# Retention's weights behind the gathers, the residual rows normalised in retention, the router's scores made as columns

## The reference

```python
x = _layernorm(x + mamba(x)); x = _layernorm(x + cross_attention(x, ctx))
x = _layernorm(x + _L0_ffn_ref(x, ...))      # switch experts
x = _layernorm(x + _L1_attn_ref(x, ...))     # retention and feed-forward
...
def _L0_ffn_ref(inputs, Wr, br, W1, b1, W2, b2):
    logits = x @ Wr + br                     # 800 tokens, 8 experts
    probs = jax.nn.softmax(logits, axis=-1)
    gate, idx = jnp.max(probs), jnp.argmax(probs)
    pos = ...                                # place in the expert, capacity 100
    expert_in = gate * x[tokens of the expert]
    eo = relu(expert_in @ W1 + b1) @ W2 + b2
    return gate * eo[expert, place]
def _L1_attn_ref(x, ...):
    xn = _ln(x, norm1_w, norm1_b)
    q, k, v = xn @ wq + bq, xn @ wk + bk, xn @ wv + bv
    ret = ((q @ k.T) * Dmat) @ v             # by head, 16 heads
    h = (silu(xn @ wg + bg) * groupnorm(ret)) @ wo + bo
    x = x + h
    x2 = _ln(x, norm2_w, norm2_b)
    return x + (silu(u) * g @ w_out + b_out) # u, g halves of x2 @ w_in + b_in
```

## Time and profile before

| what | value |
|---|---|
| time, median of 3 runs | 2862.91 us (2861.91 to 2865.08) |
| time of the profiled execution | 2860.79 us |
| its span | 2858.7 us |
| PE busy | 2504.8 us (88%) |
| PEld busy | 1266.9 us (44%) |
| DVE busy | 1393.4 us (49%) |
| ACT busy | 897.5 us (31%) |
| POOL busy | 573.4 us (20%) |
| granted clock of PE, mean | 0.938 of 2.4 GHz |

### The profile page before, as it was taken

The page is one execution under the profiler, slowest core; times in us unless marked ns, Lnnn a source line. Parts: engine busy times, 40 slices in busy tenths (PEclk is TensorE's granted clock), DMA queues, the critical chain, the costliest instruction groups (busy, mean ns, idle before and its releaser), DMA issues. The chain is left out here.

```text
span 2858.7 us, 33018 instructions
## 1 busy us (share of the span) xinstructions
PE 2504.8 (88%) x12353; PEld 1266.9 (44%) x12353; DVE 1393.4 (49%) x1981; ACT 897.5 (31%) x1867; POOL 573.4 (20%) x490
## 2 busy tenths in 40 slices
PE   7899999988999999897289899885997669999994
PEld 4544444434555555545145454353664323333331
DVE  5788888721578886721325512285444521111113
ACT  3644544402533334401012110085333112212210
POOL 0055555500000000001401100000000033343343
PEclk9999999999999999998699899997998879999997
DMA  2022222136535544335510010112000151560633
GB/s 86 25 72 82 75 85 79 66 87 244 184 113 185 173 140 120 126 110 196 147 79 0 0 41 3 32 59 89 1 1 1 54 233 50 234 265 23 261 101 116
DMA packets 94622, 288.64 MB, mean 101 GB/s; under 512 B 26994, under 2 KB 57358, under 8 KB 80258
## 3 DMA queue, kind: packets, MB, share of 16 engines
q1 hardware_dynamic: 59378, 158.34, 16.6%
q0 software_dynamic: 35104, 128.36, 12.5%
HBM read 449.40 MB, written 47.11 MB: 174 GB/s over the span
## 5 line engine op out<-in xcount | busy, mean ns | idle before, releaser
L691 POOL TENSOR_TENSOR x_rows<-ms_state,mb_C_everywhere 128x800 f32<-128x800 f32 x128 | 241.4, 1886 | 312.2 <-DVE ms_state L668 181.9
L701 PE MATMUL psum<-ms_context,mb_key_w 128*128 128x361 f32 x768 | 269.1, 486 | 22.9 <-ACT x_rows L611 9.6
L922 PE MATMUL psum<-at_Wv,at_context 128*128 128x512 f32 (+1 forms) x576 | 266.1, 601 | 0.0
L668 DVE TENSOR_TENSOR_SCAN ms_state<-ms_decay,psum 128x800 f32<-128x800 f32 x128 | 232.1, 1814 | 57.5 <-ACT ms_decay L618 41.3
L2733 PE MATMUL psum<-tf_W,tf_x_T 128*64 128x512 f32 x1024 | 232.3, 601 | 8.9 <-DMA tf_W<-in_L_W,tt_weight_row 8.9
L2755 PE MATMUL psum<-tf_W,tt_hidden 128*64 128x512 f32 x1024 | 226.8, 595 | 0.0
L2788 ACT ACTIVATE tt_hidden<-psum,tf_b 128x64 f32<-128x64 f32 x512 | 112.1, 330 | 363.7 <-PE psum L2744 363.7
L701 PEld LDWEIGHTS psum<-ms_context,mb_key_w 128*128 128x128 f32 x768 | 136.3, 190 | 162.6 <-ACT x_rows L606 64.1
L2678 POOL DMA_INDIRECT tf_W<-in_L_W,tt_weight_row x128 | 127.2, 993 | 230.7 <-PE psum L2733 151.5
L1023 ACT ACTIVATE at_prob<-psum,at_neg_max 100x722 f32<-100x722 f32 x128 | 110.5, 864 | 145.7 <-DVE at_neg_max L1085 145.4
L1085 DVE TENSOR_REDUCE at_neg_max<-psum 100x1 f32<-100x722 f32 x128 | 115.5, 903 | 78.3 <-PE psum L943 77.9
(11 more groups left out here) (461 smaller groups left out, 3876.3 us busy)
## 6 DMA issues: line engine op xcount, KB each, us to landing
at_piece<-in_L_W_f POOLq DMA_DIRECT2D x24, 1024.0 KB, 6.2
keys_dram<-x_rows SPq DMA_DIRECT2D x128, 180.5 KB, 1.9
at_k_cols<-keys_dram SPq DMA_DIRECT2D x64, 361.0 KB, 3.1
sf_W<-in_L_W SPq DMA_DIRECT2D x16, 1024.0 KB, 6.9
tf_W<-in_L_W SPq DMA_DIRECT2D x8, 2048.0 KB, 27.0
ms_context<-in_ctxT SPq DMA_DIRECT2D x16, 541.5 KB, 4.3
at_context<-in_ctxT SPq DMA_DIRECT2D x8, 1083.0 KB, 5.3
ternary_dram<-at_piece_made POOLq DMA_DIRECT2D x14, 512.0 KB, 4.0
```

The lines of the kernel that those rows point to most:

```text
L668: nc.vector.tensor_tensor_scan(state[:, n % RH, :], decay[:, g % RA, :, :].rearrange("p b l -> p (b l)"), drive[:, n % RD, :], 0.0, ALU.mu ...
L691: nc.gpsimd.tensor_tensor(seen[:, n % RH, :], state[:, n % RH, :], cC[:, n, :], ALU.mult).then_inc(weighed, 1)
L701: last = nc.tensor.matmul(side[:, 0:SH], lhsT=wk[:, k, e * P:(e + 1) * P], rhs=keys[:, h, k, :], start=(k == 0), stop=(k == KC - 1))
L922: last = nc.tensor.matmul(bank[0:rows_of(t), :], lhsT=ctxT[:, b % 2, k, t * P:t * P + rows_of(t)], rhs=wv[:, k, h * BANK:(h + 1) * BANK], ...
```

## The change

Three edits, in switch_route, in gather_cols and in retain.

1. The router's scores are made the other way round: the 8 columns of Wr are the weights and 400 columns of c.xT are streamed (two halves x 4 feature groups, 8 matmuls) into two banks, experts on partitions. ACT copies each half into a new tile logit_cols, and PE transposes it, sequence by sequence, into the bank that DVE read before.
2. In gather_cols SP waits for all eight gathers before it calls early. The tiles mv and rstd are now allocated in retention, so that they outlive the block, and POOL no longer normalises c.x.
3. In retain DVE normalises one sequence of c.x behind each odd unit, before it adds bo to it.

```diff
@@ switch_route @@
+    logit_cols = sb("logit_cols", [NE, T])
     def tensor(pe):
         pe.wait_ge(wr_loaded, 16)
+        for h in range(2):
+            for k in range(KD):
+                last = nc.tensor.matmul(c.banks[h][0:NE, 0:HALF], lhsT=wr[:, k, :], rhs=c.xT[:, k, h * HALF:(h + 1) * HALF],
+                                        start=(k == 0), stop=(k == KD - 1))
+            last.then_inc(scored, 1)
         for b in range(NB):
-            for k in range(KD):
-                last = nc.tensor.matmul(score[:, b, :], lhsT=c.xT[:, k, b * L:(b + 1) * L], rhs=wr[:, k, :],
-                                        start=(k == 0), stop=(k == KD - 1))
+            pe.wait_ge(score_cols, b // HB + 1)
+            last = nc.tensor.transpose(score[:, b, :], logit_cols[:, b * L:(b + 1) * L], c.ident[0:NE, 0:NE])
         last.then_inc(logits, 1)
     def scalar(act):
+        for h in range(2):
+            act.wait_ge(scored, h + 1)
+            nc.scalar.copy(logit_cols[:, h * HALF:(h + 1) * HALF], c.banks[h][0:NE, 0:HALF]).then_inc(score_cols, 1)
         act.wait_ge(shifted, 1)
@@ gather_cols @@
             sp.dma_start(vec[:, :, :], dram["L1_vec"]).then_inc(vec_loaded, 16)
+            for b in range(NB):
+                sp.wait_ge(y_loaded[b], 16)
             early(sp)
...
             own(nc.gpsimd.tensor_tensor(rstd[:, :], rstd[:, :], power[:, :], ALU.pow))
-            pool.wait_ge(normed, NB)
-            for b in range(NB):
-                nc.gpsimd.tensor_scalar(c.x[:, b, :], c.x[:, b, :], mv[:, b, 0:1], rstd[:, b:b + 1], ALU.subtract, ALU.mult).then_inc(once, 1)
-            pool.wait_ge(once, NB)
@@ retain, vector @@
                 dve.wait_ge(rows_loaded, 64)
-                nc.vector.tensor_tensor(x1[:, u // 2, :], c.x[:, u // 2, :], bo[:, :], ALU.add).then_inc(x_biased, 1)
+                b = u // 2
+                nc.vector.tensor_scalar(c.x[:, b, :], c.x[:, b, :], mv[:, b, 0:1], x_rstd[:, b:b + 1], ALU.subtract, ALU.mult).then_inc(x_normed, 1)
+                dve.wait_ge(x_normed, b + 1)
+                nc.vector.tensor_tensor(x1[:, b, :], c.x[:, b, :], bo[:, :], ALU.add).then_inc(x_biased, 1)
```

More of the change, by code:

```diff
@@ L1318, in switch_route @@
     in_slot, what = sb("in_slot", [L, NB, CAP]), sb("what", [L, NB, 2, NE])
-    wr_loaded = sem("Wr_loaded")
+    logit_cols = sb("logit_cols", [NE, T])
+    wr_loaded, scored, score_cols = sem("Wr_loaded"), sem("scored"), sem("score_cols_ready")
     loaded, logits, shifted, exped = sem("loaded"), sem("logits"), sem("shifted"), sem("exped")
@@ L1545, in early, with gather_cols @@
                     sp.dma_start(w[n][:, :, :], dram["L1_w" + n]).then_inc(w_loaded[n], 16)
-            gather_cols(c, gate, row, y_dram, vec, w_in, early)
-            retain(c, vec, x1, w, w_loaded, rows, rows_loaded, [(w_in, "L1_w_in"), (b_in, "L1_b_in")])
+            mv, rstd = sb2("mean_var", [L, NB, 2]), sb2("x_rstd", [L, NB])
+            gather_cols(c, gate, row, y_dram, vec, w_in, early, mv, rstd)
+            retain(c, vec, x1, mv, rstd, w, w_loaded, rows, rows_loaded, [(w_in, "L1_w_in"), (b_in, "L1_b_in")])
         normed_cols(c, "re_norm2", x1, vec, 4, None)
         feed_forward(c, vec, x1, w_in, b_in)
-def gather_cols(c, gate, row, y_dram, vec, free, early):
+def gather_cols(c, gate, row, y_dram, vec, free, early, mv, rstd):
     nc, dram = c.nc, c.dram
@@ L1563, in gather_cols @@
         y = free[0:L].rearrange("p k n -> p (k n)")[:, 0:NB * D].rearrange("p (b d) -> p b d", b=NB)
-        xn, stats, mv = sb("normed_twice", [L, NB, D]), sb("stats", [L, NB, 6]), sb("mean_var", [L, NB, 2])
-        rstd, both, power = sb("rstd", [L, NB]), sb("both_rstd", [L, NB]), sb("minus_half", [L, NB])
+        xn, stats = sb("normed_twice", [L, NB, D]), sb("stats", [L, NB, 6])
+        both, power = sb("both_rstd", [L, NB]), sb("minus_half", [L, NB])
         y_loaded = [sem(f"y_loaded_{b}") for b in range(NB)]
         summed, var_ready, chain_p = sem("vector_chain"), sem("var_ready"), sem("gpsimd_chain")
-        both_ready, normed, vec_loaded, once = sem("both_rstd_ready"), sem("rows_normed"), sem("vectors_loaded"), sem("x_normed")
+        both_ready, normed, vec_loaded = sem("both_rstd_ready"), sem("rows_normed"), sem("vectors_loaded")
         turned = Banks(c.banks[4:8], sem("turned_filled"), [sem("turned_drained_s"), sem("turned_drained_v")])
@@ L1687, in _, with retain @@
                 last.then_inc(turned.done(b), 1)
-def retain(c, vec, x1, w, w_loaded, rows, rows_loaded, later):
+def retain(c, vec, x1, mv, x_rstd, w, w_loaded, rows, rows_loaded, later):
     nc, dram = c.nc, c.dram
@@ L1706, in retain @@
         later_loaded, cleared = sem("later_loaded"), sem("cleared")
-        copied, x_biased = sem("copied"), sem("x_biased")
+        copied, x_biased, x_normed = sem("copied"), sem("x_biased"), sem("x_normed")
         scored, decayed, weighed, retained = sem("scored"), sem("decayed"), sem("weighed"), sem("retained")
```

## The result

The changed kernel took 2837.49 us (median of four runs, 2836.59 to 2841.90) beside 2863.99 us for the kernel before in the same comparison (2861.91 to 2866.83): ratio 0.991, 95% interval 0.9893 to 0.9927. The forecast was 2832.7 in a range of 2827.5 to 2840. The kernel is faster, and its time lies inside the range, 4.8 us above the forecast itself. The profiled execution took 2837.65 us (span 2835.9), against 2860.79 (span 2858.7): the span is 22.8 us shorter.

What follows compares the result with a forecast made beforehand. PE is busy in most of the span but waits on slow gathers, POOL's normalisation at the block's end and the router: 14.5 + 13.7 + 2.0 = 30.2 us off 2862.91 gives 2832.7, range 2827.5 to 2840.

Steps and rivals of the forecast that it cites:

- The gathers: In gather_cols, with SP's loads held back, the eighth row reaches DVE at 1393.6 instead of 1408.10: 14.5 us saved.
- Rival (b): Gathers stay slow from reading rows just stored, not from loads beside them: 2838.2 to 2847.2 us, chance 0.08.
- The block's end: Without POOL's normalisations, second bn_aggr to PE's q takes 9.34 us, as at normed_cols, instead of 23.03: 13.7 saved.
- What takes their place: In retention, DVE's eight normalisations hide in its waits for PE and the later loads arrive in time: cost 0.
- Rival (c): DVE's normalisation in retention shows on the path: 2833.3 to 2837.1 us, chance 0.04.
- Rival (d): Weights land too late and PE waits for wq at q's start; 60 us landing gives 2881; chance 0.03.
- The 17 us put down for the row loads: At retention's start, wq, wk and row loads land by 1410, as 0.54 of wo's 30.6 us; DVE wants them about 1413.
- The spare banks: In retention, if row loads hold DVE, PE has banks to fill for 18.9 us after q's start.
- The router: In switch_route, 16 passes of 400 columns take 5.55 us and DVE's first routing step starts 2.0 us earlier.
- I take full clock: Router passes priced at 2.4 GHz, since the clock was 1.00 until 1280 and fell during the now removed 8-column passes.
- Rival (a): Router at half clock: 2836.4 us if it falls as now, 2838.3 if down at once; chance 0.11.
- Starts from the same barriers and moves as a whole: Everything behind (retention's loop, feed-forward, ternary, top-2) keeps its length, shifting by what is saved; q's clock rise may differ.

Runs made afterwards that it cites:

- only_gathers: The kernel before with only SP's loads held back until the eight gathers land; POOL's normalisation and router old: 0.9961, median 2852.22 us.
- early_qk: The changed kernel with wq and wk issued ahead of the gathers again, the other seven loads behind them: 0.9907 of the kernel before.
- norm_five: The changed kernel with each of DVE's eight normalisations in retention made five times: 0.9898 of the kernel before, median 2835.89 us.
- after_again: The changed kernel, unchanged, compared once more with the kernel before: 0.9903, median 2833.46 us.
- only_norm: The changed kernel without SP's wait for the gathers and with the old router, so only the normalisation moved: 0.9951 of the kernel before.
- only_router: The kernel before with only the changed kernel's router (wide matmuls, ACT's copies, transposes): 1.000 over twelve runs.
- warm_route: The changed kernel plus unread matmuls where PE pauses, at the projection's end and through the routing: 0.9866 of the kernel before, median 2826.93 us.

## Why the prediction was right, and where it was off

**The gathers, right.** Forecast 14.5 us, measured 14.6; the landing of 3.9 taken from sf_x came out as 4.1. One thing differs from the picture: POOL's issues were taken to run as before, 9.29 us from first to last; they took 10.14, with single issues of up to 1.47 us where DVE now works beside them. It cost nothing that shows: DVE takes the eighth row without a wait. Rival (b) falls with only_gathers and early_qk.

**The block's end, right.** 13.7 forecast from normed_cols, 13.4 measured; 9.34 became 9.62.

**What takes their place, right.** Rival (c): norm_five. Rival (d): wq landed 4.9 us after its issue, at 1403.7, 6.2 us before q; the row loads held DVE once for 0.98 us, and PE not at all. The 17 us put down for the row loads were too few, as DVE went on 20.2 us after wq's issue: the 30.6 of wo that they were taken from count from wo's own issue, which in before came 3.9 us behind wq's. The spare banks that the prediction counted on covered it. The Trainium skill, Trainium Kernel Development and Optimization, Best Practices, asks to overlap DMA with compute; here loads taken out of an overlap made the kernel faster (only_gathers), because the stage they overlapped was itself waiting for DMA.

**The router, wrong.** This is the term that was mis-sized: 2.0 us forecast, 1.1 in the profile after, -0.1 in after_again. The step that failed is "I take full clock". The earlier trace rows shows 1.00 until 1280 in one execution, and I read the fall as due to the 8-column passes. By the stretches of 2 us it fell 0.5 to 1.5 us ahead of the router's first pass in only_gathers, after, after_again, early_qk and norm_five (mean 0.86, 0.96, 0.67, 0.62 and 0.60 in the stretch where it fell), with the old router or the new, so that its passes can't be the cause there; in before and only_norm (0.66 and 0.55) it fell 2.0 us into the old router, and what made it fall there stays open. Among the kernels without fillers only_router's alone has it at 1.00 to the router's end. At equal clock the form is worth what was forecast or somewhat more (2.6 us, or 1.6 to 2.9); what failed is the clock that it would be met with. Rival (a) with its chance of 0.11 was close to what usually happens, though not at its price: it left the clock low to the end, where in fact it rises while the 400-column passes run, so that the way to DVE took 8.0 to 9.4 us, and not the 10.9 or 12.8 that (a) made of it. That the first comparison's 2837.49 lies in (a)'s 2836.4 to 2838.3 is therefore chance: the router's part of the miss is 0.9 us, and after_again's median is 2833.46. The trace of before had a nearer price in a row that I did not read. The top-2 router there has this form already, and takes 8.2 us from its first pass to DVE, with the clock at 0.50 at its start, though PE had waited 3.75 us for a DMA there and 0.84 at this router:

```profile
2274.33 7.02 PE L2529 MATMUL psum<-x_cols,tr_Wr 128*8 128x400 f32 x16 [3.75 <-DMA tr_Wr<-in_L_Wr]
...
2281.92 0.36 PE L2534 MATMUL psum<-ident,tt_hidden 8*100 8x8 f32 x4 [0.28 <-ACT tt_hidden L2551]
...
2282.53 0.16 DVE L2560 COPY tr_logit<-psum 100x64 f32<-100x64 f32 x1
```

That would have given 9.13 - 8.2 = 0.9 us, near what after showed.

**The rest of the 4.8 us, not a term of the sum.** With 14.6, 13.4 and 1 the sum is 29, against a forecast of 30.2. after_again's 0.9903 is 27.8 us of 2862.78 (22.9 to 32.4) and holds it; the first comparison's 0.991, 25.8 (20.9 to 30.6), holds it too. What lay between is the spread of untouched stages: by the marks of the twelve profiles the router starts anywhere from 1278.6 to 1284.3 us, and PE's first scores to the end takes 1370.2 to 1383.4. "Starts from the same barriers and moves as a whole" was right on average, (that last stretch is 1377.6 us in the mean of the four profiles without the whole change, and 1375.4 in that of the eight with it), but a profile of one execution can't fix it to better than some 5 us either way, and the forecast's own 2828 to 2836 was too narrow for that: the first comparison's median lies outside it, after_again's inside.

## What to carry to other kernels

When a stage waits for many small gathers, look at which other DMAs are under way meanwhile: a bulk load that nobody needs yet is better issued behind them, if its landing time fits the gap to its first reader. When work is moved off the engine that ends a block, price it by another block of the same kernel that already ends that way; when an operation is re-formed, first look for the same form elsewhere in the trace, with the clock that it was granted there. And give a term that hangs on the clock two prices, with the odds taken from more than one execution.

## What the runs showed of the hardware

- **The clock under the two routers.** In before PE ran 8-column passes without a gap from 1280 to 1286 us; the granted clock was 0.66, then 0.50 and 0.50 in the three stretches of 2 us, and still 0.50 at 1294 (the stretches behind the earlier trace rows stand below). In after it was 0.50 when the 400-column passes began and 1.00 before they ended. The prediction had priced no such difference: once low, the clock was to stay low to the router's end. The Trainium skill, TensorE: Matmul & The Clock Gate, Part 1 (What's actually happening), has the throttled level as the default that activity releases; after agrees with it, and before shows a stretch in which PE worked all the time and nothing was released.

```profile
1282.00:1284.00 2.00, 2.00 (x13) 0.50 0.00 0
1284.00:1286.00 2.00, 2.00 (x13) 0.50 0.00 0
1294.00:1296.00 2.00, 1.58 (x10) 0.50 0.02 4
```

- **The executions of one kernel differ by some 11 us.** only_router's twelve runs spread from 2856.27 to 2867.79, warm_route's four from 2820.32 to 2831.37. The profiles show part of why: the first expert's way to the gathers is 72.6 us where the clock lasted and 76.1 where it fell, in one and the same kernel. A part worth 2 us shows in its own stretch, not in the total.
- **POOL's issue of one of these gathers** took 1.01 to 1.08 us when DVE was idle and up to 1.47 when it worked beside it (early_qk's eight: 1.01 to 1.08; after's: 1.01 to 1.47; in before only the eighth met DVE, and it took 1.42, the others 1.01 to 1.07). Some issues beside DVE stay at 1.07, and no run tests what makes the longer ones.
